# Dense stage and fourth pass of a four-layer graph network: reciprocal roots by one power instruction on GpSimd, and a sum moved within DVE's unit

## Chip, cores and metric

One core of a Trainium2 chip runs the whole program. The metric is the device time of one execution in microseconds, the median of several runs. Engines: PE (TensorE), DVE (VectorE), ACT (ScalarE), POOL (GpSimd) and SP (SyncE, which here only issues DMAs). All run their own instruction streams in order and meet at semaphores.

## What is computed

Four graph layers on 50000 nodes of 256 features and 25000 edges, each x = x + layer(relu(layernorm(x))). Layer 0 is two graph attention layers, layer 1 dot-product attention over edges, layer 2 a hyperbolic attention layer, layer 3 a two-step graph convolution. Cut to what the change touches:

```
def _layernorm(x, eps=1e-05):
    return (x - mean(x)) / sqrt(var(x) + eps)
...
# layer 2
h_dir = h_raw / maximum(norm(h_raw), 1e-12)
h_mag = sigmoid(x @ mag_w.T + mag_b) * 1.5
h = h_dir * h_mag
...
h_combined = h + agg                      # agg: softmax-weighted sum over the edges of a node
un_c = maximum(norm(h_combined), 1e-15)
h_poincare = tanh(un_c) * h_combined / un_c     # then clipped to norm 0.95
```

A reciprocal root is thus needed per row: of the layernorm's variances, and of the squared norm of h_raw and of h_combined.

## The kernel before

**The dense stage** (from line 613) treats every node as if it had no incoming edge, so that all four layers become products of rows; nodes with edges are mended afterwards. It goes over the nodes in 98 units (U = 98) of 512 rows (G = 4 rows for each of 128 partitions). It is a software pipeline: in unit n of an engine's stream, `a`, `z`, `b`, `c`, `d`, `e`, `f` are the units n, n-1, ... n-6, each at a later step of the network. `hold(engine, semaphore, value, ...)` is a wait. Each engine's unit is written out in a fixed order.

- DVE, unit n (the inner `unit`, lines 998 to 1050 or so): oo of n-6 (L1004: x3o plus a constant row, the result of nodes without edges, into its own buffer); bn_stats of xin of unit n+1 (L948, the x statistics); `scales` of n-5, which waits for ACT's tanh (reciprocals from L202 on), and x3o (L1013); em (L1018); g (L1023); two evacuations into f2o (L995), x1 (L1031) and its bn_stats (L1035); the squared norms into var (L955, which waits for ACT's squares); then `statistics` (the variance, L221 to L229, and `rsqrt`, eleven operations L150 to L163, between which the two evacuations into f1o are woven, also L995); `shifts` (nm, L967, which ACT's layernorms wait for); `norms` (L177 to L192, up to unc, which the tanh reads).
- `rsqrt` (lines 146 to 165) makes a first value by an integer shift and subtraction and improves it in three steps of three operations. It writes rt, 12 values for each partition here; ACT takes rt as its scale, with nm as its bias. Its last step scales by ROOT = 16, since var holds the sum and not the mean of the squares.
- ACT: h1 of n (L885, the first reader of nm and rt), the copy hr (L895), zm (L900), the turned copies tt (L874), tanh of n-5 (L906), exp (L909), h2 of n-3 (L914), squares of n-4 (L923), ho (L932).
- PE: transposes (L820) and products (L830) for three of the steps.
- POOL, unit n: for n < 28 an iota and seven indirect DMAs into PLACE (`scatter_places`, L779 and L784), afterwards six small gathers (`find_places`, L796); then `fetch_targets`, two gathers of rows of x into xd (L768), which wait until the XD store of unit n-2 has landed.
- SP, unit n, in this order, each entry behind its own wait: store F1 of n-1 (waits for f1o), store HL of n-6 (ho), store `out` of n-6 (oo), store X3 of n-5 (x3o), store H2 of n-3, store F2 of n-2 (f2o), load xin of unit n+2 (L700: waits until h1 and x1 of unit n-2 have freed the slot; there are four), store XD of n-2 (L740). The stores are of 512 to 528 KB, XD's of 256 KB, the load of 512 KB. The core lines of SP's unit:

```
j = at.back(6)
...
    hold(sp, s["oo"], j.n + 1, ps)
    sp.dma_start(view, flat(oo, j.slot, np_)).then_inc(o_out[j.slot], 16)
...
if at.back(-2).alive(U):
    load(at.back(-2))
```

**The fourth pass** (from line 2183) goes over the 25088 padded edges in 28 groups of seven tiles of 128 and computes the softmax-weighted sums of layer 2. POOL gathers group n's rows of HL (seven indirect DMAs, L1318, into one of three slots); the gather of n waits until PE has accumulated group n-3. DVE, group n: lg (L2306, waits for the gathered rows), crow and the selection (L1438) of n-1, two scans (L1386, L1388) of n, then for n-3 var (L2324), `rsqrt` and unc (L2326), then hc of n-2 (L2336), the differences of n, and the output of n-3 (L2350), which waits for ACT's tanh of unc. PE, ACT and SP serve the same groups.

Of the kernel before, what the change touches and what calls it, by code (L numbers as in the profile page):

```python
# [172 lines left out]
def magnitude(nc, link, fac, e, r, un, unc, n2):  # L173
# [11 lines left out]
    n = link.go(V.scalar_tensor_tensor(fac, fac, 1.5 / ROOT, r, ALU.mult, ALU.mult))  # L185
    yield
    link.need(n)
    if un is not None:
        n = link.go(V.tensor_tensor(un, un, fac, ALU.mult))
        yield  # L190
        link.need(n)
        n = link.go(V.tensor_scalar(unc, un, 1.0 / ROOT, 1e-15, ALU.mult, ALU.max))  # L192
        yield
        link.need(n)
# [20 lines left out]
def layernorm_stats(nc, link, st, mean, dm, var):  # L215
# [15 lines left out]
    link.need(n)  # L231


def gnn_program(nc, x, src, dst, edge_weight, W1, a_src1, a_dst1, b1, W2, a_src2, a_dst2, b2,
# [36 lines left out]
    with ctx:  # L271
# [341 lines left out]
        with Phase() as ph:  # L613
# [16 lines left out]
            var, ra = ph.sb("var", [P, 3 * G]), ph.sb("ra", [P, 3 * G])  # L630
# [19 lines left out]
                "f1_h", "f2_h", "hr_h", "em", "sq", "x1", "unc", "tanh", "x3", "ho", "oo", "warm", "pad", "low", "edge")}  # L650
# [39 lines left out]
            with nc.Block() as block:  # L690
# [61 lines left out]
                def _(pool):  # L752
                    pp = ph.passed["pool"]
                    nc.gpsimd.memset(ho[:, :, :, 258:F2W], 1.0)
                    nc.gpsimd.iota(low_i[:, :], [[1, 1]], base=N - P, channel_multiplier=1)
                    nc.gpsimd.memset(warm[:, :], 0.0).then_inc(s["pad"], 1)
# [43 lines left out]

                    def unit(at):
                        if at.n < NS:
                            scatter_places(at.n)
                        else:
                            find_places(at.n - NS)
                        fetch_targets(at.n)
                    unrolled(pool, U, 0, unit)
# [130 lines left out]
                def _(dve):  # L938
# [18 lines left out]
                    def statistics(at):  # L957

                        yield from layernorm_stats(nc, link, st, mean[:, :], dm[:, :], var[:, 0:2 * G])
                        hold(dve, s["h1_h"], min_int(at.n * 2, 2 * U), pv)  # L960
                        hold(dve, s["h2"], min_int(at.n - 3, U), pv)
                        yield from rsqrt(nc, link, rt[:, at.slot, :], var[:, :], ra[:, :], ROOT)

                    def shifts(at):

                        if at.back(-1).alive(U) or at.back(2).alive(U):
# [3 lines left out]
                    def norms(at):  # L970
# [5 lines left out]
                                             un[:, :], unc[:, :], n2[:, d.slot, :])  # L976
# [11 lines left out]
                    take(statistics(At(-1, -1, 3, 4)))  # L988
# [9 lines left out]
                    def unit(at):  # L998
                        a, z, b, c, d, e, f = (at.back(k) for k in range(7))
                        link.restart()  # L1000
                        if f.alive(U):
                            hold(dve, s["x3"], f.n + 1, pv)
                            hold(dve, o_out[f.slot], 16 * f.use, pv)
                            V.tensor_tensor(oo[:, f.slot, :, :], x3o[:, f.slot, :, :], wide(gcn_const, D, G),  # L1004
                                            ALU.add).then_inc(s["oo"], 1)
# [503 lines left out]
        def within(n):  # L1509
            return 0 <= n < NS  # L1510
# [672 lines left out]
        with SoftPass(1, 1, 259, (HL, 7), None, X3) as ph:  # L2183
            ph.step("scaled", "hc", "sq", "unc", "tanh", "tiles_turned", "tile_sums", "sums_turned", "tile_carry", "carry_turned",
# [6 lines left out]
            var, ra, rt = ph.sb("var", [P, GS]), ph.sb("ra", [P, GS]), ph.sb("rt", [P, GS])  # L2191
# [67 lines left out]
            with nc.Block() as block:  # L2259
                @block.gpsimd  # L2260
                def _(pool):
                    ph.start_pool(pool)
# [5 lines left out]
                    every(0, group)  # L2268
# [25 lines left out]
                def _(dve):  # L2294
# [5 lines left out]
                    def group(n):  # L2300
# [464 lines left out]
```

## Time and profile before

| | us |
|---|---|
| median of 3 runs | 5989.73 |
| lowest, highest run | 5988.09, 6006.96 |
| span of the profiled execution (its own device time is not listed apart) | 5993.1 |
| PE busy in the span | 4608.6 (77%) |
| DVE busy | 4603.5 (77%) |
| POOL busy | 3500.3 (58%) |
| ACT busy | 2965.7 (49%) |

The profile is of one execution; its times are microseconds from the start of the span. "L995" is line 995. Busy time excludes waits and the issuing of DMAs by SP. In a row of the timeline stand the start, the duration, the engine, the line and operation, the tiles (out<-in) with their sizes, how many instructions were merged (x4), and in brackets how long the engine had been idle before and what released it. SPq rows are DMA issues: their duration is the issue, not the transfer.

### The profile page before, as it was taken

How to read it: one execution, taken by the hardware profiler on the slowest of the kernel's cores; microseconds unless marked ns; L12 is line 12 of the kernel's file. 1: busy time of each engine (PE TensorE's matmuls, PEld its weight loads, DVE VectorE, ACT ScalarE, POOL GpSimd, SP SyncE). 2: the span in 40 equal slices, each digit the busy share in tenths (PEclk: the TensorE clock that was granted, in tenths of full speed). 3: DMA queues.
4: the chain of work that ended last, by engine and by line, in shares of the span. 5: the costliest groups of instructions: out<-in, count | busy, mean ns of one | idle time of the engine just before them, and what ended most of it. 6: DMA issues, size and time to landing. Idle time of an engine off the chain costs nothing. (4 is left out here: it accounts for less than half of the span.)

```text
span 5993.1 us, 77451 instructions
## 1 busy us (share of the span) xinstructions
PE 4608.6 (77%) x21160; PEld 3351.9 (56%) x21160; DVE 4603.5 (77%) x13478; ACT 2965.7 (49%) x7524; POOL 3500.3 (58%) x3009
## 2 busy tenths in 40 slices
PE   3888888888884888865777778888857674887887
PEld 3666666666663666643565545555534443665555
DVE  5888888888886888847999647777768887985554
ACT  2777777777772444432444435555545552331111
POOL 3555445454524767728888278777725433546777
PEclk9999999999996999987888889999978887998998
DMA  3666666667663444425777535555536774554444
GB/s 119 239 242 247 237 243 241 244 242 244 240 236 128 125 123 129 128 71 174 256 243 250 200 110 155 147 151 155 154 103 217 249 241 151 169 159 132 140 156 130
DMA packets 651621, 1096.83 MB, mean 183 GB/s; under 512 B 88390, under 2 KB 471814, under 8 KB 651069
## 3 DMA queue, kind: packets, MB, share of 16 engines
q1 hardware_dynamic: 525754, 837.10, 41.0%
q0 software_dynamic: 125440, 254.79, 14.7%
q8 instruction: 176, 2.88, 0.2%
q14 instruction: 251, 2.06, 0.1%
HBM read 523.88 MB, written 575.95 MB: 184 GB/s over the span
## 5 line engine op out<-in xcount | busy, mean ns | idle before, releaser
L830 PE MATMUL mm<-w,tt 128*128 128x264 f32 x3136 | 736.9, 389 | 0.8 <-ACT tt L874 0.8
L830 PEld LDWEIGHTS mm<-w,tt 128*128 128x128 f32 x3136 | 585.5, 192 | 92.5 <-ACT tt L874 1.0
L1318 POOL DMA_INDIRECT aim<-F,index x392 | 551.7, 1407 | 119.5 <-issue 119.2
L768 POOL DMA_INDIRECT xd<-in_x_dram,index x196 | 218.4, 1114 | 676.0 <-DMA XD<-xd 645.1
L1318 POOL DMA_INDIRECT got<-F,index x392 | 491.9, 1255 | 204.7 <-issue 111.2
L1476 ACT ACTIVATE rows<-acc 128x260 f32<-128x260 f32 (+1 forms) x588 | 227.4, 387 | 623.4 <-PE acc L1467 623.4
L796 POOL DMA_INDIRECT place<-PLACE,place_ix x392 | 425.2, 1085 | 119.5 <-issue 119.5
L820 PE MATMUL tp<-ident,h 128*128 128x128 f32 x1568 | 236.8, 284 | 323.9 <-ACT h L914 162.0
L1463 PE MATMUL acc<-got,sel 128*128 128x260 f32 (+1 forms) x1176 | 425.8, 449 | 74.8 <-DVE sel L1438 68.2
L2487 DVE SCALAR_TENSOR_TENSOR agg<-mask,agg,acc 128x128 f32<-128x128 f32 x784 | 251.8, 343 | 253.5 <-PE acc L2474 144.2
L830 PE MATMUL mm<-wl,tt 128*128 128x264 f32 x1568 | 419.4, 389 | 6.0 <-ACT tt L874 5.8
L820 PEld LDWEIGHTS tp<-ident,h 128*128 128x128 f32 x1568 | 167.5, 141 | 426.5 <-ACT h L885 224.3
L1208 PE MATMUL kv<-wkv,ht 128*128 128x512 f32 x784 | 384.9, 615 | 0.1
L885 ACT ACTIVATE h<-xin,nm,rt 128x256 f32<-128x256 f32 x392 | 203.3, 589 | 325.2 <-DVE nm L967 325.2
L874 ACT ACTIVATE tt<-tp 128x512 f32<-128x512 f32 x588 | 314.4, 585 | 79.3 <-PE tp L820 79.3
L1467 PE MATMUL acc<-rows,carry 128*128 128x260 f32 (+1 forms) x1008 | 345.0, 426 | 7.9 <-ACT rows L1476 1.7
L1318 POOL DMA_INDIRECT got<-HL,index x196 | 216.0, 1102 | 225.9 <-PE acc L1467 173.3
L1376 PE MATMUL turned<-ident,top 128*4 128x128 f32 (+1 forms) x588 | 124.9, 380 | 283.0 <-DVE top L1368 151.5
L1463 PEld LDWEIGHTS acc<-got,sel 128*128 128x128 f32 x1176 | 250.2, 225 | 142.4 <-DVE sel L1438 82.2
L2738 ACT ACTIVATE yt<-m,b_col 128x512 f32<-128x512 f32 x98 | 67.5, 689 | 504.4 <-PE m L2714 504.4
L830 PEld LDWEIGHTS mm<-wl,tt 128*128 128x128 f32 x1568 | 260.5, 192 | 83.2 <-issue 9.2
L2442 POOL DMA_INDIRECT got<-X,index x196 | 196.6, 1003 | 180.5 <-ACT h L2609 134.7
(348 smaller groups left out, 13645.7 us busy)
## 6 DMA issues: line engine op xcount, KB each, us to landing
F<-f1o SPq DMA_DIRECT2D x97, 528.0 KB
F<-f2o SPq DMA_DIRECT2D x97, 528.0 KB, 3.4
HL<-ho SPq DMA_DIRECT2D x97, 528.0 KB, 3.7
xin<-in_x_dram SPq DMA_DIRECT2D x97, 512.0 KB
H<-h SPq DMA_DIRECT2D x97, 512.0 KB, 3.7
X<-x3o SPq DMA_DIRECT2D x97, 512.0 KB
out_dram<-oo SPq DMA_DIRECT2D x97, 512.0 KB
drow<-DSTF SPq DMA_DIRECT2D x84, 448.0 KB
```

The costliest lines, as they stand in the source:

```text
L768: nc.gpsimd.indirect_dma_start(out=xd[:, n % 2, t, :], out_offset=None, in_=x, in_offset=bass.IndirectOffsetOnAxis(ap=index[:, tile, 1:2], ...
L796: nc.gpsimd.indirect_dma_start(out=place[:, t, k:k + 1], out_offset=None, in_=cells, in_offset=bass.IndirectOffsetOnAxis(ap=place_ix[:, t, ...
L820: last = nc.tensor.transpose(bank[:, 2 * r + k, :], rows_t[:, 2 * q + r, k * P:(k + 1) * P], ident[:, :])
L830: last = nc.tensor.matmul(mm[PAIR[stage, q]][:, r, 0:F2W], lhs[:, q, 2 * r + k, :], w[:, k, :], start=(k == 0), stop=(k == KB - 1))
L874: nc.scalar.activation(tt[k][:, q, :, :], tp[q][:, :, :], ACT.Copy).then_inc(s["t_h"], 1)
L885: relu = nc.scalar.activation(h1[:, r, :], xin[:, a.slot4, r, :], ACT.Relu, bias=nm[:, last_turn, r:r + 1], scale=rt[:, last_turn, r:r + 1])
L1208: last = nc.tensor.matmul(acc, lhs[:, k, :], w[:, k, :], start=(k == 0), stop=(k == KB - 1))
L1318: nc.gpsimd.indirect_dma_start(out=buf[:, n % SLOTS, t, :], out_offset=None, in_=table, in_offset=bass.IndirectOffsetOnAxis(ap=index[:, n ...
L1463: nc.tensor.matmul(acc, self.sel[:, s, t, :], self.got[:, n % SLOTS, t, 0:w], start=True, stop=False)
L1467: nc.tensor.matmul(acc, self.carry[:, s, t * P:(t + 1) * P], self.rows[:, s, t - 1, :] if t else self.crow[:, :], start=False, stop=True)\
L1476: nc.scalar.activation(self.rows[:, n % 2, t, :], self.acc[tile % 2][:, 0:self.width], ACT.Copy)\
L2487: last = nc.vector.scalar_tensor_tensor(self.agg[:, sl, k, t * P:(t + 1) * P], self.mask[:, sl, t, :], before, self.acc[sl][:, t, k, :], A ...
```

## The change

In the dense stage and in the fourth pass `rsqrt` goes. DVE signals a new semaphore `var` when the variances stand; POOL has a tile `half` of -0.5 and computes rt = var ^ -0.5 by one tensor_tensor instruction with the operation pow (128 x 12 values in the dense stage, 128 x 7 in the fourth pass), and signals `root`, for which DVE waits before nm (dense stage) or unc (fourth pass). In the dense stage a `variance` function gives the mean of the squares in place of their sum, so the factor ROOT becomes 1. oo moves from the head of DVE's unit to behind the f1o evacuations, ahead of nm; SP's stream stays as it is. POOL's `roots(n)` stands between its place work and `fetch_targets`, and in the fourth pass the power of group n-3 stands behind gather(n).

```diff
+def variance(nc, link, st, mean, dm, var, ready):
+    V = nc.vector
+    V.tensor_tensor(mean, st[:, :, 1], st[:, :, 4], ALU.add)
+    n = link.go(V.tensor_tensor(dm, st[:, :, 1], st[:, :, 4], ALU.subtract))
+    link.go(V.scalar_tensor_tensor(var, st[:, :, 2], D * 1e-5, st[:, :, 5], ALU.add, ALU.add))
+    link.need(n)
+    n = link.go(V.scalar_tensor_tensor(dm, dm, 0.25, dm, ALU.mult, ALU.mult))
+    link.need(n)
+    V.scalar_tensor_tensor(var, var, 1.0 / D, dm, ALU.mult, ALU.add).then_inc(ready, 1)
...
 # dense stage, POOL
+                    nc.gpsimd.memset(half[:, :], -0.5)
...
+                    def roots(n):
+                        hold(pool, s["h1_h"], min(n * 2, 2 * U), pp)
+                        hold(pool, s["h2"], min(n - 3, U), pp)
+                        hold(pool, s["var"], n + 2, pp)
+                        nc.gpsimd.tensor_tensor(rt[:, n % 2, :], var[:, :], half[:, :], ALU.pow).then_inc(s["root"], 1)
+
                     def unit(at):
                         if at.n < NS:
                             scatter_places(at.n)
-                        else:
+                        elif at.n < U:
                             find_places(at.n - NS)
+                        roots(at.n)
                         fetch_targets(at.n)
-                    unrolled(pool, U, 0, unit)
+                    roots(-1)
+                    unrolled(pool, U, 6, unit)
...
 # dense stage, DVE
-                    def statistics(at):
-                        yield from layernorm_stats(nc, link, st, mean[:, :], dm[:, :], var[:, 0:2 * G])
+                    def statistics():
+                        variance(nc, link, st, mean[:, :], dm[:, :], var[:, 0:2 * G], s["var"])
+
+                    def shifts(at):
                         hold(dve, s["h1_h"], min_int(at.n * 2, 2 * U), pv)
                         hold(dve, s["h2"], min_int(at.n - 3, U), pv)
-                        yield from rsqrt(nc, link, rt[:, at.slot, :], var[:, :], ra[:, :], ROOT)
-                    def shifts(at):
+                        hold(dve, s["root"], at.n + 2, pv)
...
                     def unit(at):
                         a, z, b, c, d, e, f = (at.back(k) for k in range(7))
                         link.restart()
-                        if f.alive(U):
-                            hold(dve, s["x3"], f.n + 1, pv)
-                            hold(dve, o_out[f.slot], 16 * f.use, pv)
-                            V.tensor_tensor(oo[:, f.slot, :, :], x3o[:, f.slot, :, :], wide(gcn_const, D, G),
-                                            ALU.add).then_inc(s["oo"], 1)
                         if at.back(-1).alive(U):
                             x_stats(at.back(-1))
...
-                        steps = statistics(at)
+                        statistics()
                         if a.alive(U):
                             hold(dve, f1_out[a.slot], 16 * a.use, pv)
                             for q in range(2):
-                                take(steps, 5)
                                 evacuate(a, "a", "mma_h", f1o[:, a.slot, :, 0:F2W], rb1, "f1_h", q)
-                        take(steps)
+                        if f.alive(U):
+                            hold(dve, s["x3"], f.n + 1, pv)
+                            hold(dve, o_out[f.slot], 16 * f.use, pv)
+                            V.tensor_tensor(oo[:, f.slot, :, :], x3o[:, f.slot, :, :], wide(gcn_const, D, G),
+                                            ALU.add).then_inc(s["oo"], 1)
                         shifts(at)
...
 # fourth pass, POOL
                     def group(n):
                         if within(n):
                             ph.gather(pool, n, 0, bound, d["acc"], (n - 2) * GS)
-                    every(0, group)
+                        c = n - 3
+                        if within(c):
+                            hold(pool, d["unc"], c, None)
+                            hold(pool, d["var"], c + 1, None)
+                            nc.gpsimd.tensor_tensor(rt[:, :], var[:, :], half[:, :], ALU.pow).then_inc(d["root"], 1)
+                    every(3, group)
...
 # fourth pass, DVE
-                            link(V.tensor_scalar(var[:, :], n2[:, c % 2, :], 1e-30, None, ALU.max))
-                            take(rsqrt(nc, link, rt[:, :], var[:, :], ra[:, :]))
-                            V.tensor_tensor(unc[:, :], var[:, :], rt[:, :], ALU.mult).then_inc(d["unc"], 1)
+                            V.tensor_scalar(var[:, :], n2[:, c % 2, :], 1e-30, None, ALU.max).then_inc(d["var"], 1)
...
                             hold(dve, d["hc"], x + 1, None)
                             dve.sem_inc(d["used"], 1)
+                        if within(c):
+                            hold(dve, d["root"], c + 1, None)
+                            V.tensor_tensor(unc[:, :], var[:, :], rt[:, :], ALU.mult).then_inc(d["unc"], 1)
```

## Rows read from the trace of the kernel before

**Rows 1.** The page: busy time of each engine (share of the span).

```profile
PE 4608.6 (77%) x21160; PEld 3351.9 (56%) x21160; DVE 4603.5 (77%) x13478; ACT 2965.7 (49%) x7524; POOL 3500.3 (58%) x3009
```

**Rows 2.** Busy time by stretch: PE, PEld, DVE, ACT, POOL; then clock, DMA share, GB/s.

```profile
600.00:1200.00 600.00, 492.40 (x2586) 390.28 (x2585) 511.95 (x1736) 456.87 (x1089) 297.75 (x274) 1.00 0.69 242
...
4530.00:4980.00 450.00, 297.61 (x1160) 190.28 (x1159) 392.26 (x1155) 226.27 (x786) 177.82 (x162) 0.79 0.72 236
```

**Rows 3.** Timeline of one dense unit, ACT and DVE.

```profile
1001.15 2.07 ACT L885 ACTIVATE h<-xin,nm,rt 128x256 f32<-128x256 f32 x4 [3.27 <-DVE nm L967]
...
1002.59 1.24 DVE L1004 TENSOR_TENSOR oo<-x3o,gcn_const 128x1024 f32<-128x1024 f32 x1 [0.36 <-DVE unc L192]
...
1006.01 0.20 ACT L906 ACTIVATE th<-unc 128x4 f32<-128x4 f32 x1
...
1006.25 0.18 DVE L202 RECIPROCAL gb<-unc 128x4 f32<-128x4 f32 x1 [1.11 <-ACT th L906]
...
1015.07 0.17 DVE L229 TENSOR_TENSOR var<-dm,var 128x8 f32<-128x8 f32 x1
...
1015.56 0.70 DVE L995 TENSOR_TENSOR f1o<-mm,rb 128x528 f32<-128x528 f32 x1
...
1018.51 0.17 DVE L967 SCALAR_TENSOR_TENSOR nm<-mean,rt 128x8 f32<-128x8 f32 x1
```

**Rows 4.** Timeline, DVE: oo of the unit 34 units earlier.

```profile
401.75 1.23 DVE L1004 TENSOR_TENSOR oo<-x3o,gcn_const 128x1024 f32<-128x1024 f32 x1 [0.36 <-DVE unc L192]
```

**Rows 5.** Timeline of SP's queue in the same unit.

```profile
1003.85 0.34 SPq L719 DMA_DIRECT2D out_dram<-oo  x1
1009.22 0.32 SPq L724 DMA_DIRECT2D X<-x3o  x1
...
1012.97 0.33 SPq L700 DMA_DIRECT2D xin<-in_x_dram  x1
1013.34 0.63 SPq L740 DMA_DIRECT2D XD<-xd  x1
```

**Rows 6.** GpSimd: groups by line (busy us, mean ns, idle before), and one timeline row.

```profile
L1318 POOL DMA_INDIRECT got<-HL,index x196 | 216.0, 1102 | 225.9 <-PE acc L1467 173.3 <-issue 51.8 <-DVEq L1308 0.8
L784 POOL DMA_INDIRECT PLACE<-edge_row,index x196 | 209.5, 1069 | 59.4 <-issue 51.3 <-POOL edge_row L779 8.1
...
L755 POOL IOTA low_i<- 128x1 int32 x1 | 0.1, 134 | 0.0
...
1019.52 1.00 POOL L768 DMA_INDIRECT xd<-in_x_dram,index  x1 [6.95 <-DMA XD<-xd]
```

**Rows 7.** Busy time by stretch, columns as in rows 2: two single microseconds.

```profile
1002.00:1003.00 1.00, 0.65 (x4) 0.42 (x4) 0.64 (x2) 1.00 (x3) 0.69 (x2) 1.00 1.00 410
1009.00:1010.00 1.00, 0.82 (x8) 0.83 (x9) 1.00 (x3) 0.81 (x4) 0.81 (x1) 1.00 0.02 1
```

**Rows 8.** Timeline of the first load and its reader; landing of XD's stores (L740's view).

```profile
75.69 1.30 SPq L700 DMA_DIRECT2D xin<-in_x_dram  x3
...
79.24 1.41 DVE L948 BATCH_NORM_STATS2 st<-xin 128x6 f32<-128x256 f32 x4 [3.23 <-DMA xin<-in_x_dram]
...
DMA to landing us min/median/max: 3.2/5.2/5.9
```

**Rows 9.** Timeline of the fourth pass, POOL and DVE.

```profile
4509.62 1.00 POOL L1318 DMA_INDIRECT got<-HL,index  x1 [7.61 <-PE acc L1467]
...
4518.87 1.24 POOL L1318 DMA_INDIRECT got<-HL,index  x1 [0.30 <-issue]
...
4523.28 0.17 DVE L2306 TENSOR_TENSOR lg<-got,aim_score 128x7 f32<-128x7 f32 x1 [1.31 <-DMA got<-HL,index]
...
4540.24 0.17 DVE L2306 TENSOR_TENSOR lg<-got,aim_score 128x7 f32<-128x7 f32 x1 [0.18 <-issue]
4546.45 0.13 DVE L2324 TENSOR_SCALAR var<-n 128x7 f32<-128x7 f32 x1
```

**Rows 10.** Line 2324 (var of the fourth pass): durations, first and last start.

```profile
L2324 DVE TENSOR_SCALAR var<-n x28: 132/132/173, 4528.9 to 4972.0; 128x7 f32<-128x7 f32 x28
```

More of the change, by code:

```diff
@@ L170, in min_int, with magnitude @@
     return min(value, most) if type(value) is int else value
-def magnitude(nc, link, fac, e, r, un, unc, n2):
+def magnitude(nc, link, fac, e, r, un, unc, n2, root=ROOT):
     V = nc.vector
@@ L184, in magnitude @@
     link.need(n)
-    n = link.go(V.scalar_tensor_tensor(fac, fac, 1.5 / ROOT, r, ALU.mult, ALU.mult))
+    n = link.go(V.scalar_tensor_tensor(fac, fac, 1.5 / root, r, ALU.mult, ALU.mult))
     yield
@@ L191, in magnitude @@
         link.need(n)
-        n = link.go(V.tensor_scalar(unc, un, 1.0 / ROOT, 1e-15, ALU.mult, ALU.max))
+        n = link.go(V.tensor_scalar(unc, un, 1.0 / root, 1e-15, ALU.mult, ALU.max))
         yield
@@ L629, in gnn_program @@
             mean, dm = ph.sb("mean", [P, 2 * G]), ph.sb("dm", [P, 2 * G])
-            var, ra = ph.sb("var", [P, 3 * G]), ph.sb("ra", [P, 3 * G])
+            var, half = ph.sb("var", [P, 3 * G]), ph.sb("half", [P, 3 * G])
             rt, nm = ph.sb("rt", [P, 2, 3 * G]), ph.sb("nm", [P, 2, 2 * G])
@@ L649, in gnn_program @@
                 "ch", "stats", "h1_h", "h2", "zm", "exp", "g", "tp_h", "t_h", "mma_h", "mmb_h", "mmc_h",
-                "f1_h", "f2_h", "hr_h", "em", "sq", "x1", "unc", "tanh", "x3", "ho", "oo", "warm", "pad", "low", "edge")}
+                "f1_h", "f2_h", "hr_h", "em", "sq", "x1", "unc", "tanh", "x3", "ho", "oo", "warm", "pad", "low", "edge", "ones", "var", "root")}
             def rows_of(table, at):
@@ L975, in norms @@
                         yield from magnitude(nc, link, fac[:, d.slot, :], em[:, d.slot, :], rt[:, at.slot, 2 * G:3 * G],
-                                             un[:, :], unc[:, :], n2[:, d.slot, :])
+                                             un[:, :], unc[:, :], n2[:, d.slot, :], 1.0)
                     def scales(e):
@@ L987, in _ @@
                     link.restart()
-                    take(statistics(At(-1, -1, 3, 4)))
+                    statistics()
                     shifts(At(-1, -1, 3, 4))
@@ L1037, in unit @@
                         link.restart()
-                        steps = statistics(at)
+                        statistics()
                         if a.alive(U):
@@ L2183, in gnn_program @@
         with SoftPass(1, 1, 259, (HL, 7), None, X3) as ph:
-            ph.step("scaled", "hc", "sq", "unc", "tanh", "tiles_turned", "tile_sums", "sums_turned", "tile_carry", "carry_turned",
+            ph.step("scaled", "hc", "sq", "var", "root", "unc", "tanh", "tiles_turned", "tile_sums", "sums_turned", "tile_carry", "carry_turned",
                     "filled", "filled_turned")
@@ L2190, in gnn_program @@
             den, n2, th = ph.sb("den", [P, GS]), ph.sb("n2", [P, 2, GS]), ph.sb("th", [P, GS])
-            var, ra, rt = ph.sb("var", [P, GS]), ph.sb("ra", [P, GS]), ph.sb("rt", [P, GS])
+            var, half, rt = ph.sb("var", [P, GS]), ph.sb("half", [P, GS]), ph.sb("rt", [P, GS])
             unc = ph.sb("unc", [P, GS])
@@ L2261, in _ @@
                 def _(pool):
+                    nc.gpsimd.memset(half[:, :], -0.5)
                     ph.start_pool(pool)
```

## The prediction, made before the change was run

> **What bounds the kernel now.** I read the engine totals first: DVE and TensorE are each busy 77% of the span and no engine is full, so no sum of busy time decides [rows 1]. Next the busy times by stage. The dense stage (about 79 to 1860 us) repeats one unit 98 times plus a few to fill and drain; between 600 and 1200 us DVE is busy 512 of 600 us, and in the fourth pass (about 4480 to 4980) 392 of 450 [rows 2]. There DVE is nearly the bound, so the waits around it matter. The third view is one unit in order of time [rows 3]. It shows a loop of two engines. ACT waits 3.27 us for nm, the shifts that end DVE's unit. From its first operation behind nm (1001.15) ACT works without a pause to the tanh, which ends at 1006.21: 5.1 us. DVE waits 1.11 us for it and then works from 1006.25 to the next nm at 1018.51. The eleven root operations and the two f1o evacuations (0.70 each) stand in the 3.27 us between var's end (1015.24) and nm. oo, the sum that the change moves, stands just behind the norms, at 1002.59, where it and the x statistics fill the time until the tanh. From the oo of 401.75 to that of 1002.59 are 34 units: 17.67 us each [rows 4, 3].
>
> The view of SP's own queue is the fourth and decides the forecast [rows 5]. SP works in order. In its unit n it stores F1 and HL, waits for oo of this same unit n of DVE (the out store, n-6), and only behind that stores X3, H2 and F2, **loads xin for unit n+2**, and stores XD. Now out goes at 1003.85, early in the unit, and the load at 1012.97, when x1 has freed its slot. DVE unit n+1 begins with the statistics of exactly that load.
>
> **The change in the dense stage.** (1) Eleven root operations leave DVE. (2) oo comes between f1o and nm. What stands between var and nm becomes two evacuations of 0.70 and oo with 1.23 (0.70 + 0.70 + 1.23 = 2.63), against 3.27: 0.64 us less per unit, if nothing else moves. DVE behind nm is left with norms and statistics and waits longer for the tanh, which costs nothing as that is ACT's chain. (3) The power on GpSimd runs beside these 2.63 us. No row shows it. Its lower bound is 0.13 us, GpSimd's smallest iota; an indirect DMA's issue, which works through 128 rows, takes 1.07 to 1.10 [rows 6]; nothing excludes several times that for a transcendental function, so I set 4 us as the upper end, my choice, four times that issue. I take 1.0, near the indirect DMA's issue, as that row too is more than a memory write. In the dense stage it is free up to 2.6 us. GpSimd reaches it in time: at unit n its place gathers are issued by 1012.6, var ends at 1015.24, and GpSimd waits for XD's store until 1019.52 anyway (its row has 6.95 us of wait) [rows 3, 6].
>
> (4) The queue that oo is moved past is SP's. The out store now waits for the end of DVE's unit, and X3, H2, F2, the xin load and XD all stand behind it, though their data is ready. Call the end of oo T. The issues are 0.37 us apart [rows 5], so the load is issued at T + 1.5, about where nm is. Four stores go ahead of it into the DMA engines. The X3 store that was issued at 1009.22 left the engines idle until about 1009.97 (their share is 0.02 in the microsecond from 1009), and full engines move some 400 GB/s (410 in the microsecond from 1002) [rows 5, 7], so 528 KB take 1.3 us. The engines begin at T + 0.75 and are through the four stores at T + 0.75 + 5.2 = T + 5.95. The load's own data and receipt: the first load of the stage, issued at 75.69, let DVE start at 79.24, so 3.55 us of which 0.75 before data moves, 2.8. In the steady units XD, issued 0.37 behind the load, lands at a median of 5.2 [rows 8], 5.6 behind the load's issue; less some 1.3 for XD's own 256 KB in small rows the load lands 4.3 behind its issue, and some 0.8 of that is the wait for F2's data ahead of it: 3.5 or less. I take 3.35: **the load lands at T + 9.3** (bounds 8.2 to 10.5). Then: statistics 1.4 [rows 8], 0.1 to the first reciprocal, and from there (1006.25) to var's end (1015.24) 8.99, then 2.63. The new loop is 9.3 + 1.4 + 0.1 + 8.99 + 2.63 = **22.4 us against 17.67, 4.75 more**. It holds where there is both an out store and a load, units 6 to 95: 90 x 4.75 = +428 us. The 14 units around them gain 0.64 each, -9.
>
> Does something else then bind? XD lands 1.3 to 2 behind the load, at about T + 11, GpSimd's two target gathers take 2.6 more, its seven scatters of the first 28 units (1.07 and 0.3 of issue each) and their iota 9.9 [rows 6]: it reaches the next power at T + 23.5, 1.1 us behind the next oo. nm would be late by some 2 us, but the tanh (5.1 behind nm) is still ready before the statistics at the next T + 10.7. TensorE keeps its 14.5 us of work a unit (492.4 over 34) [rows 2]. So no.
>
> **The change in the fourth pass.** Eleven operations of 0.2 us leave each of 28 groups (2.2 us). But GpSimd's group n issues gather(n), then waits for var of DVE's group n, then the power, and only then gather(n+1). Today gathers run ahead, held only by TensorE's accumulation: at 4509.62 one starts that way, its seventh issue is at 4518.87 and DVE's lg had to wait for the data until 4523.28 [rows 9]. Now gather(n+1) starts behind var of group n, and group n+1 begins with lg. From lg to var's end are 6.34 us (4540.24 to 4546.58), power 1.0, from the first of seven issues to the last 8.75 (six steps of 1.10 and 0.30 are 8.4 [rows 6], the row's case with one slow one has 9.25), landing behind the last 4.4 (4518.87 to 4523.28): 20.5 us against a mean of 16.41 (var from 4528.9 to 4972.0 over 27 intervals) [rows 9, 10]. 24 gathers (4 to 27) are held: 24 x 4.1 = +98. Bounds: with a landing of 2.8 (the first load's above) and a power of 0.13, 18.0 a group, +39; with 4 us of power +170. The last groups have no gather and gain 2 us each, -6. The new waits in DVE's group stand behind 3.4 us of hc and cost nothing.
>
> **Sum.** +428 - 9 + 98 - 6 = +511. The profile's span is 5993.1, 3.4 above the median of 5989.7, less than the 0.3% (18 us) that a measurement here tells from no change; against the median I forecast 6500.
>
> **What the Trainium skill adds.** Row and page on the DMA: "DMA: Bandwidth & Descriptors", on the anatomy of one DMA, gives some 2.0 us fixed plus bytes over 436 GB/s. That is, as an estimate, T + 8.0 for four stores and a load, and the sum would be about 117 us smaller. The first load's 3.55 us agrees with its 3.2 within 0.4. On the power: "GPSIMD Engine Reference", performance versus the Vector engine, has elementwise work on GpSimd at about half DVE's speed, which speaks against moving it; twice the 0.17 us of a DVE root operation would make the fourth pass 16 us shorter than my sum.
>
> **Rivals.** (a) The load does not queue behind the stores' data and lands as it does in the steady units, about 4.3 after its issue, T + 5.9. The loop is then 5.9 + 13.1 = 19.0, +1.35 x 90 = +122, in all 6195. For it: reads and writes are different traffic. Against it: XD, half the size, lands at a median of 5.2 behind the load and at 3.2 at its quickest [rows 8]. 9%.
> (b) The power takes about 4 us and holds oo back, since both read SBUF: oo ends at var + 5.2 in place of + 2.63, 2.6 x 90 = +234, and the fourth pass 3 x 24 = +72: 6805. It decides from 1.4 us, when f1o is done and oo would start; its point is that oo then delays SP's queue too. Whether GpSimd and DVE hold each other up so, no row of this kernel shows, and its price is unseen. 7%. "SBUF — State Buffer", on who interferes with whom, states such a lock between a DVE operation with two SBUF inputs and a GpSimd operation that reads SBUF; f1o reads PSUM and is not concerned.
> (c) Faster: SP's queue costs nothing, the load lands before the tanh is ready anyway. For this it must land by T + 3.7, 2.2 us after its issue. Then -0.64 x 98 = -63; if the gathers of the fourth pass also stay ahead, 28 x 2.2 = -62: 5865. Against it: the shortest landing of an XD store is 3.2, and the first load, with nothing ahead, took 3.55 [rows 8]. 3%.
> (d) Parts of both cancel (small dense loss, gather loss alone), within 0.3%: 2%.
>
> **How the numbers follow.** My forecast, 6500, holds 79%. Its range adds the ends of the load's landing (-1.1 and +1.2 us x 90 = -99 and +108) and of the fourth pass (-59 and +72, power included): 6342 to 6680. With a part of (b) above and the coarse rates below I give 6340 to 6700; (a) and (c) lie outside. Faster 0.03, same 0.02, slower 0.95.
>
> **What would show it.** After: nm to nm 22.4 us in the dense stage (units 6 to 95), the x statistics (L948 now) waiting for the DMA of xin, 5 us or so in each, in place of the wait for the tanh; SP's out, X3, H2, F2, xin and XD issued within 2.5 us at the end of DVE's unit; the engines idle for nearly half the unit; the power under 2.6 us. In the fourth pass: lg waiting for got, and gathers whose first issue follows the power, groups of about 20.5. Units below 19.5 us would make the queueing wrong; a power above 2 us the price; nm still waited for by ACT at 17 us a unit, the whole argument.

## The result: slower by 9.5%, and the profile after

The changed kernel took a median of 6566.61 us (6558.91 to 6571.59, 4 runs), the kernel before beside it 5991.31: a ratio of 1.095, 95% interval 1.0935 to 1.0966. The forecast was 6500 in a range of 6340 to 6700.

The page of the profiled execution, engine totals, against [rows 1]:

```profile
PE 4777.6 (73%) x21160; PEld 3452.8 (53%) x21160; DVE 4359.9 (66%) x12015; ACT 2967.0 (45%) x7524; POOL 3831.4 (58%) x3144
```

DVE did 244 us less work, GpSimd 331 more, and the kernel is 577 us longer: the time went into waits. The busy times of the stretch from 600 to 1200 us, as in [rows 2], show DVE down from 512 to 356 of 600 us (TensorE's granted clock fell from 1.00 to 0.91 in it; in the view of waits from 200 to 2200 us DVE waits for PE nowhere, so the lower clock doesn't set the unit):

```profile
600.00:1200.00 600.00, 442.73 (x2044) 340.78 (x2042) 356.11 (x1077) 359.41 (x859) 317.45 (x249) 0.91 0.53 190
```

The last oo of the dense stage starts at 2273.4 us, before it was 1851.1: 422 us later. The fourth pass adds the rest. The view of oo's line and of var's line in the fourth pass, after (count, durations, first and last start), against [rows 10]:

```profile
L1064 DVE TENSOR_TENSOR oo<-x3o,gcn_const x98: 1212/1216/1223, 190.3 to 2273.4; 128x1024 f32<-128x1024 f32 x98
...
L2351 DVE TENSOR_SCALAR var<-n x28: 132/133/172, 4943.1 to 5550.8; 128x7 f32<-128x7 f32 x28
```

A group of the fourth pass is (5550.8 - 4943.1) / 27 = 22.51 us long, before 16.41, together +165 us. With the 422 that is 587, ten more than the whole, which the other stages give back.

The timeline of one dense unit after, the counterpart of [rows 3] and [rows 5], with SP's issues between DVE's and GpSimd's work (T is the end of oo, as in the prediction):

```profile
1003.54 1.41 DVE L971 BATCH_NORM_STATS2 st<-xin 128x6 f32<-128x256 f32 x4 [5.57 <-DMA xin<-in_x_dram]
...
1013.68 0.17 DVE L244 SCALAR_TENSOR_TENSOR var<-var,dm 128x8 f32<-128x8 f32 x1
1013.76 1.32 DVE L1018 TENSOR_TENSOR f1o<-mm,rb 128x528 f32<-128x528 f32 x2
1014.12 1.01 POOL L810 DMA_INDIRECT place<-PLACE,place_ix  x1 [0.30 <-DVE var L244]
1015.00 1.22 DVE L1064 TENSOR_TENSOR oo<-x3o,gcn_const 128x1024 f32<-128x1024 f32 x1
1015.15 3.21 POOL L820 TENSOR_TENSOR rt<-var,half 128x12 f32<-128x12 f32 x1
1016.24 0.34 SPq L732 DMA_DIRECT2D out_dram<-oo  x1
1016.62 0.43 SPq L737 DMA_DIRECT2D X<-x3o  x1
1017.10 0.78 SPq L742 DMA_DIRECT2D H<-h  x1
1017.92 1.18 SPq L747 DMA_DIRECT2D F<-f2o  x1
1018.50 0.17 DVE L990 SCALAR_TENSOR_TENSOR nm<-mean,rt 128x8 f32<-128x8 f32 x1 [2.29 <-POOL rt L820]
...
1019.20 1.14 SPq L713 DMA_DIRECT2D xin<-in_x_dram  x1
...
1020.38 1.20 SPq L753 DMA_DIRECT2D XD<-xd  x1
...
1026.16 1.40 DVE L971 BATCH_NORM_STATS2 st<-xin 128x6 f32<-128x256 f32 x4 [6.58 <-DMA xin<-in_x_dram]
```

The reader sees the queue. oo ends at 1016.22 (T). SP issues its store and right behind it four transfers that waited for nothing but their turn. The load is the fifth in the row, goes out at T + 2.98, and the statistics that read it begin at 1026.16, T + 9.94, after 6.58 us of waiting. One loop is 22.6 us (1003.54 to 1026.16). This unit is longer than most: over the 88 units whose statistics start between 176 and 2139 us the mean is 22.3 us, and from T to the statistics the median is 9.35 us, 3.0 to the load's issue and 6.4 from there. Before, a unit is 17.6 us by the same measure.

The transfers' data starts only behind T. The DMA share, last column but one, of two single microseconds of this unit (columns as in [rows 2]); between them, from 1017 on, it is 0.94 or more in each:

```profile
1016.00:1017.00 1.00, 0.86 (x5) 0.33 (x3) 0.21 (x1) 0.00 (x0) 1.00 (x1) 1.00 0.01 0
1025.00:1026.00 1.00, 1.00 (x5) 0.54 (x3) 0.00 (x0) 1.00 (x3) 0.00 (x0) 1.00 1.06 426
```

Two views of waits say the same for the stretch from 200 to 2200 us, DVE's and SP's own (us in total, times, longest):

```profile
DVE st L971 <- DMA xin<-in_x_dram: 539.2, 90, 8.6
...
DVE nm L990 <- POOL rt L820: 220.5, 90, 4.6
```

```profile
SPq L732 <- DVE oo L1064: 1387.6, 90, 17.5
```

The second line looks like a second price, the power that nm waits for. The tanh, 5.1 us behind nm, is ready at about 1023.8, before the statistics can even start. And oo, at which SP's queue starts, doesn't wait for the power. So that wait costs nothing here; the experiments show when it begins to.

The fourth pass after, one group:

```profile
5202.39 0.13 DVE L2351 TENSOR_SCALAR var<-n 128x7 f32<-128x7 f32 x1
...
5202.68 1.52 POOL L2294 TENSOR_TENSOR rt<-var,half 128x7 f32<-128x7 f32 x1 [12.13 <-DVE var L2351]
...
5204.39 1.08 POOL L1339 DMA_INDIRECT got<-HL,index  x1 [0.19 <-issue]
...
5212.50 0.37 SPq L2314 DMA_DIRECT2D xe<-XE  x1
...
5212.85 1.00 POOL L1339 DMA_INDIRECT got<-HL,index  x1 [0.30 <-issue]
...
5220.52 0.17 DVE L2333 TENSOR_TENSOR lg<-got,aim_score 128x7 f32<-128x7 f32 x1 [8.06 <-DMA got<-HL,index]
```

GpSimd is idle for 12 us until var, takes the power, then issues seven gathers, and DVE starts its next group 7.7 us after the last of them was issued (median of 19 groups: 7.4). SP's next transfers (xe, the X3 store, drow) go out at the very time of that last issue.

### The profile page after: what moved, and what is told of

Its sections match the earlier page's. It is cut to its first block and busy times, and to the rows that moved or that the text cites. A ratio compares the mean times of both kernels' runs of the same rounds, so it can differ in the third digit from the quotient of the medians.

```text
span 6569.8 us, 76354 instructions
## 1 busy us (share of the span) xinstructions
PE 4777.6 (73%) x21160; PEld 3452.8 (53%) x21160; DVE 4359.9 (66%) x12015; ACT 2967.0 (45%) x7524; POOL 3831.4 (58%) x3144
## 3 DMA queue, kind: packets, MB, share of 16 engines
q14 instruction: 242, 1.98, 0.1%
## 5 line engine op out<-in xcount | busy, mean ns | idle before, releaser
L853 PE MATMUL mm<-w,tt 128*128 128x264 f32 x3136 | 877.3, 436 | 192.1 <-DVE f2o L1018 191.8
L853 PEld LDWEIGHTS mm<-w,tt 128*128 128x128 f32 x3136 | 660.8, 219 | 346.3 <-issue 226.1
L843 PE MATMUL tp<-ident,h 128*128 128x128 f32 x1568 | 269.3, 315 | 365.0 <-ACT h L908 289.1
L971 DVE BATCH_NORM_STATS2 st<-xin 128x6 f32<-128x256 f32 x392 | 137.7, 414 | 544.1 <-DMA xin<-in_x_dram 542.6
L843 PEld LDWEIGHTS tp<-ident,h 128*128 128x128 f32 x1568 | 192.8, 157 | 462.6 <-ACT h L908 352.3
L820 POOL TENSOR_TENSOR rt<-var,half 128x12 f32<-128x12 f32 x105 | 302.3, 2879 | 74.2 <-DVE var L244 72.4
L1397 PEld LDWEIGHTS turned<-ident,top 128*4 128x4 f32 (+1 forms) x588 | 58.1, 107 | 503.2 <-DVE top L2336 309.8
```

Source lines behind the costliest of these rows:

```text
L820: nc.gpsimd.tensor_tensor(rt[:, n % 2, :], var[:, :], half[:, :], ALU.pow).then_inc(s["root"], 1)
L843: last = nc.tensor.transpose(bank[:, 2 * r + k, :], rows_t[:, 2 * q + r, k * P:(k + 1) * P], ident[:, :])
L853: last = nc.tensor.matmul(mm[PAIR[stage, q]][:, r, 0:F2W], lhs[:, q, 2 * r + k, :], w[:, k, :], start=(k == 0), stop=(k == KB - 1))
```

## Experiments

Theory A after the result: the dense loss is SP's queue behind the late oo, the fourth pass's is GpSimd's gathers behind var. Rival B: the power itself, 2.3 to 3.2 us on GpSimd, makes the loss. Rival C: DVE's own order. Each ratio is to the kernel before on the same chip, which takes 5998 us beside e1 to e4 and 5996 beside e5 to e8. e9, e10 and e11 ran on a chip where it takes 6059 us, so they are compared by their ratios. Medians of units or groups below are read from the timelines of 85 to 90 dense units, or of 18 or 19 groups in the middle of the fourth pass, which are longer than the mean over all 27 intervals (before: 16.9 against 16.4 us).

**e1_oo_head: the changed kernel, oo back at the head of DVE's unit.**

```diff
+                        if f.alive(U):
+                            hold(dve, s["x3"], f.n + 1, pv)
+                            hold(dve, o_out[f.slot], 16 * f.use, pv)
+                            V.tensor_tensor(oo[:, f.slot, :, :], x3o[:, f.slot, :, :], wide(gcn_const, D, G),
+                                ALU.add).then_inc(s["oo"], 1)
                         if at.back(-1).alive(U):
                             x_stats(at.back(-1))
...
-                        if f.alive(U):
-                            hold(dve, s["x3"], f.n + 1, pv)
-                            hold(dve, o_out[f.slot], 16 * f.use, pv)
-                            V.tensor_tensor(oo[:, f.slot, :, :], x3o[:, f.slot, :, :], wide(gcn_const, D, G),
-                                ALU.add).then_inc(s["oo"], 1)
                         shifts(at)
```

> The changed kernel with one part undone: oo back at the head of DVE's unit, the powers stay on GpSimd. Theory A (SP's queue behind oo makes the dense loss): units fall from 22.6 us to 17.2 or less, as the load is issued in mid-unit again; the fourth pass keeps its 22.5 us a group, so about 5991 + 166 - 50 = 6110 us. The power should take 2.3 us without oo beside it, nm waits for it behind f1o for about 1 us. Rival B (the power on GpSimd, late or slow, makes the dense loss): units stay above 21 us and the time above 6450.

Measured: 6081.61 us, ratio 1.0139 (1.012 to 1.0159): 485 us less than the changed kernel. The timeline of its unit, from var to oo:

```profile
1006.12 0.17 DVE L244 SCALAR_TENSOR_TENSOR var<-var,dm 128x8 f32<-128x8 f32 x1
1006.20 1.32 DVE L1018 TENSOR_TENSOR f1o<-mm,rb 128x528 f32<-128x528 f32 x2
1006.46 2.30 POOL L820 TENSOR_TENSOR rt<-var,half 128x12 f32<-128x12 f32 x1 [2.85 <-DVE var L244]
...
1008.89 0.17 DVE L990 SCALAR_TENSOR_TENSOR nm<-mean,rt 128x8 f32<-128x8 f32 x1 [1.38 <-POOL rt L820]
...
1014.20 0.18 DVE L202 RECIPROCAL gb<-unc 128x4 f32<-128x4 f32 x1 [1.25 <-ACT th L929]
```

nm starts 2.60 us behind var's end, before 3.27 [rows 3], and DVE waits for the tanh again and no longer for the load (4.7 us of idle ahead of all 392 statistics). The first loads of the two kernels differ by 1 us at most, and the last oo starts at 1798.9, before 1851.1: the powers alone make the dense stage some 52 us shorter. Units are 16.9 us, within the expectation; the total is 28 us under it. Rival B is wrong.

**e2_out_last: the changed kernel, the out store as the last issue of SP's unit.**

```diff
-                            view, np_ = rows_of(out, j)
-                            hold(sp, s["oo"], j.n + 1, ps)
-                            sp.dma_start(view, flat(oo, j.slot, np_)).then_inc(o_out[j.slot], 16)
...
                                 .then_inc(xd_out[j.slot], 16)
+                        j = at.back(6)
+                        if j.alive(U):
+                            view, np_ = rows_of(out, j)
+                            hold(sp, s["oo"], j.n + 1, ps)
+                            sp.dma_start(view, flat(oo, j.slot, np_)).then_inc(o_out[j.slot], 16)
```

> The changed kernel, oo late in DVE's unit, but SP issues the out store as the last of its unit, behind the load and XD. Theory A: the late oo itself is harmless, only the stores and the load queued behind it are dear; units 17.5 to 18.2 us, about 6130 to 6210 us in all with the fourth pass as it is. If a power that is under way holds oo back (both read SBUF), the power takes 2.3 us from var, oo comes behind it, nm about 3.8 us behind var: units 18.2. If not, nm is 3.3 or less behind var: units 17.6. Rival B (power): above 21 us a unit. Rival C (the late oo delays DVE itself, not SP): units above 20.

Measured: 6095.82 us, ratio 1.0168 (1.0149 to 1.0186). DVE's and GpSimd's streams are the changed kernel's own; the place of one store in SP's order is worth 471 us. That shows the queue, and against rival C that a late oo costs DVE nothing. The same stretch of its unit:

```profile
1004.40 0.17 DVE L244 SCALAR_TENSOR_TENSOR var<-var,dm 128x8 f32<-128x8 f32 x1
...
1004.75 2.30 POOL L822 TENSOR_TENSOR rt<-var,half 128x12 f32<-128x12 f32 x1 [2.85 <-DVE var L244]
1005.72 1.22 DVE L1066 TENSOR_TENSOR oo<-x3o,gcn_const 128x1024 f32<-128x1024 f32 x1
1006.96 0.34 SPq L757 DMA_DIRECT2D out_dram<-oo  x1
1007.18 0.17 DVE L992 SCALAR_TENSOR_TENSOR nm<-mean,rt 128x8 f32<-128x8 f32 x1 [0.24 <-POOL rt L822]
```

oo starts while the power is under way and takes its usual 1.22 us: the power does not hold oo back. nm comes 2.61 us behind var's end. The total was 34 us under the expected span, as the units did not reach 17.5 but 16.9.

**e3_move_only: the kernel before, with oo moved and nothing else.**

```diff
                         take(steps)
+                        if f.alive(U):
+                            hold(dve, s["x3"], f.n + 1, pv)
+                            hold(dve, o_out[f.slot], 16 * f.use, pv)
+                            V.tensor_tensor(oo[:, f.slot, :, :], x3o[:, f.slot, :, :], wide(gcn_const, D, G),
+                                ALU.add).then_inc(s["oo"], 1)
                         shifts(at)
```

> The kernel before with one part of the change alone: oo moved behind f1o and the last root operation, ahead of nm; roots stay on DVE. Theory A: the whole dense loss and a little more, since the eleven operations stay in the loop: units of 22.6 + 0.64 = 23.2 us, 90 x 5.5 = +500, about 6490 us; the fourth pass unchanged at 16.4 us a group. Rival B: close to 5991, at most + 120 (1.2 us a unit of oo in the path).

Measured: 6603.31 us, ratio 1.1013 (1.0987 to 1.1039), 113 us more than expected. Its last oo starts at 2458.5: the dense stage grew by 607 us, not by 500. The mechanism is the expected one, only larger, with the statistics waiting for the load:

```profile
1014.60 0.34 SPq L719 DMA_DIRECT2D out_dram<-oo  x1
...
1017.57 1.16 SPq L700 DMA_DIRECT2D xin<-in_x_dram  x1
...
1023.61 1.40 DVE L948 BATCH_NORM_STATS2 st<-xin 128x6 f32<-128x256 f32 x4 [8.07 <-DMA xin<-in_x_dram]
```

From these starts (statistics at 999.70 and 1023.61) a unit is 23.9 us, the median is 24.1; its load lands at T + 9.0. The expected 23.2 had a wrong sum behind it: it added the 0.64 us by which 3.27 (roots and evacuations) is longer than 2.63 (evacuations and oo). But here oo stands behind the 3.27, not in their place. From the statistics to the end of oo are 14.9 us (median) against 12.7 in the changed kernel: 2.2 us more a unit, over 90 units some 200 us, which is the step from 422 to 607 within 15 us.

**e4_fourth_only: the kernel before, with the fourth pass of the change.** Its diff is the fourth-pass half of the change above.

> The kernel before with only the fourth pass changed. If the parts add up: dense unchanged, the fourth pass at 22.5 us a group, 5991 + 166 = 6157 us. If part of the fourth pass's loss came from the dense stage's new timing (a later start, another clock), less than 6130.

Measured: 6146.06 us, ratio 1.025 (1.0226 to 1.0275), +148 us. Its groups are (5127.6 - 4529.9) / 27 = 22.14 us long. The parts add up: the 422 us of the dense stage and these 148 make 570, and the changed kernel is 575 us longer than the one before. The end of one of its groups:

```profile
4721.76 1.00 POOL L1318 DMA_INDIRECT got<-HL,index  x1 [0.31 <-issue]
4721.79 0.36 SPq L2293 DMA_DIRECT2D xe<-XE  x1
...
4728.56 0.17 DVE L2312 TENSOR_TENSOR lg<-got,aim_score 128x7 f32<-128x7 f32 x1 [6.79 <-DMA got<-HL,index]
```

**e6_gate_only: the kernel before, GpSimd waits for var but takes no power.**

```diff
                             ph.gather(pool, n, 0, bound, d["acc"], (n - 2) * GS)
-                    every(0, group)
+                        c = n - 3
+                        if within(c):
+                            hold(pool, d["var"], c + 1, None)
+                    every(3, group)
...
                             link(V.tensor_scalar(var[:, :], n2[:, c % 2, :], 1e-30, None, ALU.max))
+                            dve.sem_inc(d["var"], 1)
```

> The kernel before with one thing added in the fourth pass: GpSimd waits behind gather(n) for var of group n-3, as in the change, but takes no power; the roots stay on DVE. Theory A (the place of the wait costs, not the power): the group is 22.5 less the power's 1.5 = 21.0 us, 5998 + 24 x 4.6 = 6108 us. Rival (the power costs): close to 5998.

Measured: 6025.36 us, ratio 1.0051 (1.0033 to 1.007), +30 us where 110 were expected. Groups of (5007.3 - 4529.7) / 27 = 17.69 us. Both sides were wrong: the gate costs 1.3 us a group, and the power's 1.5 us alone cannot make up the other 4.4. The timeline shows what differs from e4:

```profile
4720.93 1.00 POOL L1318 DMA_INDIRECT got<-HL,index  x1 [0.30 <-issue]
4723.06 0.36 SPq L2290 DMA_DIRECT2D xe<-XE  x1
...
4724.37 0.17 DVE L2309 TENSOR_TENSOR lg<-got,aim_score 128x7 f32<-128x7 f32 x1 [1.34 <-DMA got<-HL,index]
```

Here the last gather is issued 2.1 us ahead of SP's xe, the first of its transfers of 2.2 MB, and its data is used 3.44 us after its issue. In e4 the two coincide and it is 6.8. What closes the 2.1 us is mostly the power. Counted from lg (medians), the last gather is issued at 14.8 us in e6 and at 16.4 in e4, where the power of 1.51 us stands ahead of the gathers; xe goes out at 16.8 in e6 and at 16.3 in e4, where DVE's group has lost its eleven operations.

**e9_burst_waits: e4, and SP holds xe, the X3 store, drow and carry until the next group's gathers have landed.** Against e4:

```diff
+                        if within(n + 1):
+                            ph.gathered(sp, n + 1)
                         if within(c):
                             hold(sp, d["put"], c, None)
```

> e4_fourth_only (the fourth pass of the change alone, 22.1 us a group) with one wait more on SP: its burst of xe, the X3 store, drow and carry waits until the gathers of the next group have landed. Theory A (the gathers' late landing, 6.8 us behind the last issue in place of e6's 3.4, is the burst's data in the same DMA engines): the landing falls to 3.4 us and the group to 18.8 to 19.2 us, about 6070 us. Rival (the power or the issue itself makes the landing late): 22 us a group, 6146 us.

Measured: ratio 1.0083 (1.0058 to 1.0108) against e4's 1.025; groups of (5043.9 - 4539.6) / 27 = 18.68 us. Its last gather and the next lg:

```profile
4724.51 1.00 POOL L1318 DMA_INDIRECT got<-HL,index  x1 [0.30 <-issue]
4727.34 0.36 SPq L2295 DMA_DIRECT2D xe<-XE  x1
4727.34 0.17 DVE L2314 TENSOR_TENSOR lg<-got,aim_score 128x7 f32<-128x7 f32 x1 [3.61 <-DMA got<-HL,index]
```

2.83 us from issue to use (median 2.9, in e4 7.1). Everything ahead of that is as in e4: from lg to var's end 6.35 us, to the first gather 8.2, to the last 16.5 (e4: 16.4), so the other chip doesn't explain the difference. So of the 5.7 us that e4's group is longer than before, 3.5 are the collision with SP's transfers (22.14 - 18.68) and 1.3 the gate (e6). The remaining 1.0 is a difference between e9 and e6: the power's 1.5 us less a landing that is 0.6 us shorter than e6's. The shares hold for this order of undoing; no run holds the burst back with the gate alone.

**e7_lag_alone: the fourth pass's power one group later in GpSimd's stream, dense stage of before.** Against e4:

```diff
-                        c = n - 3
+                        c = n - 4
...
-                    every(3, group)
+                    every(4, group)
```

> The kernel before with the fourth pass's roots on GpSimd, one group later in its stream. Theory A: no loss, and DVE, busy most of the group, gives back part of the 2.2 us of its eleven operations: 14.6 to 16.4 us a group, 5945 to 5998 us.

Measured: 5995.55 us, ratio 1.0002 (0.9992 to 1.0011). The loss is gone, and nothing is gained: the groups are (4968.9 - 4525.6) / 27 = 16.42 us long. The waits from 4530 to 5000 us say where DVE's 2.2 us went:

```profile
DVE wt L1411 <- PE back L1403: 65.7, 25, 2.9
```

DVE now waits 2.6 us a group for PE's results, which stand behind the accumulations in PE's order; before it is 0.4 us. DVE was 87% busy in that stretch [rows 2], but its operations lay beside a chain of PE and ACT of the same length.

**e5_head_and_lag: both repairs, e1's dense stage and e7's fourth pass.**

> oo at the head of DVE's unit as in e1_oo_head, and in the fourth pass GpSimd takes the power one group later in its stream (behind gather(n) that of group n-4), so that the gathers stay ahead. Theory A (both losses are queues: SP's behind oo, GpSimd's gathers behind var): the dense stage keeps e1's gain of some 60 us, the fourth pass is at 15 to 16.4 us a group: 5900 to 5935 us, faster than both kernels. Rival (the gathers were late through the power's own time): the groups stay above 19 us, 6000 or more.

Measured: 5939.1 us, ratio 0.9908 (0.9893 to 0.9923), faster than both kernels and 4 us over the expected span. Its last oo starts at 1796.6, 54.5 us earlier than before; the fourth pass, with groups of (4914.3 - 4471.2) / 27 = 16.41 us, gives nothing.

**e8_split_power: e5 with the dense power in two instructions.** Against e5:

```diff
-                        nc.gpsimd.tensor_tensor(rt[:, n % 2, :], var[:, :], half[:, :], ALU.pow).then_inc(s["root"], 1)
+                        for part in (slice(0, 2 * G), slice(2 * G, 3 * G)):
+                            nc.gpsimd.tensor_tensor(rt[:, n % 2, part], var[:, part], half[:, part],
+                                                    ALU.pow).then_inc(s["root"], 1)
...
-                        hold(dve, s["root"], at.n + 2, pv)
+                        hold(dve, s["root"], at.n * 2 + 3, pv)
...
+                        hold(dve, s["root"], at.n * 2 + 4, pv)
                         if d.alive(U):
                             take(norms(at))
```

> e5 with the dense power in two instructions, first the eight variances that nm waits for, then the four norms. If the power's time goes by its columns (1.5 us for 7, 2.3 us for 12 so far), nm comes some 0.6 us earlier behind var, 98 x 0.6 = 59 us less than e5. If each power has a large fixed cost or the last norms then end the unit, no gain against e5.

Measured: 5888.92 us, ratio 0.9817 (0.9804 to 0.9831), 50 us less than e5 where 59 were expected, and the best version. Its powers by shape (busy us, mean ns), and nm:

```profile
L821 POOL TENSOR_TENSOR rt<-var,half 128x8 f32<-128x8 f32 x105 | 175.1, 1667 | 221.1 <-DVE var L244 221.1
L821 POOL TENSOR_TENSOR rt<-var,half 128x4 f32<-128x4 f32 x105 | 105.8, 1008 | 0.0
```

```profile
1009.22 0.17 DVE L244 SCALAR_TENSOR_TENSOR var<-var,dm 128x8 f32<-128x8 f32 x1
...
1011.37 0.17 DVE L992 SCALAR_TENSOR_TENSOR nm<-mean,rt 128x8 f32<-128x8 f32 x1 [0.74 <-POOL rt L821]
1012.26 0.17 DVE L177 TENSOR_SCALAR fac<-em 128x4 f32<-128x4 f32 x1 [0.73 <-POOL rt L821]
```

nm starts 1.98 us behind var's end, 0.6 less than in e1; the second part delays only the norms, which have time until the tanh.

**e10_oo_with_power: e2 with oo ahead of the f1o evacuations, so that it has begun when the power starts.** The edit moves the four lines of oo to behind `statistics()`.

> e2_out_last (units of 16.9 us, power 2.30 us) with oo ahead of the f1o evacuations, so that oo is under way when the power begins. Theory A (a GpSimd operation that reads SBUF waits for a DVE operation with two SBUF inputs that began first): the power takes 3.2 us as in the changed kernel, nm comes 0.9 us later, units 17.8 us, about 6180 us. Rival (the long power of the changed kernel had another cause, as GpSimd's preceding gathers): power 2.3 us, 6096 us.

Measured: ratio 1.0269 (1.024 to 1.0299) against e2's 1.0168. Units of 17.73 us (nm at 1010.11 and 1027.84; in e2 16.9). oo and the power:

```profile
1006.59 1.22 DVE L1062 TENSOR_TENSOR oo<-x3o,gcn_const 128x1024 f32<-128x1024 f32 x1
1006.85 3.12 POOL L822 TENSOR_TENSOR rt<-var,half 128x12 f32<-128x12 f32 x1 [2.82 <-DVE var L244]
```

The power takes 3.12 us, 0.82 more than in e2 where it began first.

**e11_load_first: the changed kernel, SP's load ahead of the out store, stores and XD still behind it.**

```diff
+                        if at.back(-2).alive(U):
+                            load(at.back(-2))
+                        if j.alive(U):
                             view, np_ = rows_of(out, j)
                             hold(sp, s["oo"], j.n + 1, ps)
...
-                        if at.back(-2).alive(U):
-                            load(at.back(-2))
```

> The changed kernel with SP's load of xin ahead of the out store, the stores and XD still behind it. Theory A: the statistics no longer wait for DMA. If nothing else binds, units of 16.9 us as in e2 and 6096 us. But XD is still late: it lands some 8.5 us behind oo, GpSimd's gathers take 10.7 more and the power 2.3 to 3.2, so nm comes 22 us behind the oo of a unit before, and 16.7 us after nm comes the next oo but one: a loop of 38.7 us over two units, 19.4 a unit, 6096 + 90 x 2.4 = 6310 us. I expect this second one.

Measured: ratio 1.0531 (1.0463 to 1.0598). The statistics no longer wait for DMA, and a second queue binds: XD late, GpSimd's gathers late, and the power at 1006.74, 4.6 us behind var. oo starts at 986.38, 1003.31 and 1024.68: units of 16.9 and 21.4 in turn, 19.2 on the mean, as the expected loop over two units says. The mean over all units, (2023.8 - 193.9) / 97 = 18.9, is 0.5 under the expected 19.4, partly as the units at both ends are short. The ratio is the expected one: 6310 over 5998 is 1.052.

## Why the prediction was right

**The dense stage, step by step.** Predicted +419 us, measured 422 at the last oo; units of 22.4, measured 22.3 on the mean. (4), SP's queue, is shown by e2, where DVE and GpSimd do the same and only SP's order differs, and by e3, where the move alone makes the loss. Its terms: the load was to be issued at T + 1.5 and went at T + 3.0, since four issues in a row take 0.34, 0.43, 0.78 and 1.18 us and not 0.37 each, a distance that the prediction took from a single pair; it was to land 7.8 behind its issue and did so 6.4 behind (medians). The two errors cancel, T + 9.3 against T + 9.35, and that the dense stage came out within 3 us is luck to that extent; the mechanism is not. The rest of the loop, 13.1 in the prediction, took 12.7 (1003.54 to the end of oo at 1016.22). The Trainium skill's "DMA: Bandwidth & Descriptors" (anatomy of one DMA), whose figures gave the estimate T + 8.0, is 1.4 us low at the median and 1.9 in the unit shown; its fit is for one DMA issued from GpSimd, and these are five in a row from SP.

(1) and (2), 0.64 us less a unit if nothing else moves, came out as e1: nm 2.60 us behind var against 3.27. But not through oo's and the evacuations' 2.63: there the power sets it.

(3), the power, was put at 1.0 us; it takes 2.30 for 12 values, and 3.21 in the changed kernel. The interval up to 4 held it, but by the prediction's own sign, a power above 2 us, its price was wrong. It was free in the dense stage, though not because it fits beside 2.6 us: nm comes 4.7 us behind var's end (median), and what pays for it is the other reason given, that the tanh is ready before the load.

**The fourth pass.** Predicted +92, measured +165: groups of 22.5 and not 20.5. The gate is there, and two of the four terms hold (lg to var's end 6.3 us, first to last issue 8.5 where 8.75 stood). The power is 1.5 and not 1.0, and the landing is the term that was mis-sized: 7.7 against 4.4. I took it from one gather of the kernel before. e9 shows that the difference is the collision with SP's burst, with 3.5 us a group, and that with it gone the landing is 2.8. What brings them together is a consequence of the change that the prediction did not draw: the power delays the last gather by 1.6 us behind lg, and SP's transfers go 0.5 us earlier, as DVE's group has lost eleven operations (e6 against e4). This term, with the power's 0.5 us, is why the total came 67 us above the forecast, inside its range. The sentence that DVE is nearly the bound there was wrong too: e7 takes the eleven operations, 2.2 us, away without loss and gains nothing, as PE's accumulations end last.

**The rivals.** (a), a load that is issued late but does not queue behind the stores' data, is out by its own numbers: it had the load land 4.3 us behind its issue and units of 19.0, and measured are 6.4 and 22.3, with the DMA engines busy from the stores' first data to the landing. e2 doesn't decide this, since it takes the wait away and the burst with it. How the 2.1 us above 4.3 divide between the stores' data, the transfers issued behind the load and the load's own longer issue (1.15 us where it is 0.33 before, medians), no run separates. (b) had the lock the wrong way round: in e2 oo starts inside the power and is not held; in e10 and in the changed kernel the power starts inside oo and takes 0.8 to 0.9 us more. "SBUF — State Buffer" of the Trainium skill (who interferes with whom) says that the one that starts first blocks the other fully; the trace agrees for a power behind oo and not for oo behind a power, and the measurement decides. (c) would have needed a load within 2.2 us. "GPSIMD Engine Reference" of the Trainium skill (performance versus the Vector engine) has its factor of about two from an add of 2048 columns. The estimate made from it, twice a DVE operation's 0.17 us, is far below the 2.30 us measured for a power of 12; its direction holds, though eleven operations of DVE, 2.2 us in their chain, are about one power.

## What to carry to other kernels

When an operation moves later on its engine, look at the queue of the engine that waits for it: here one store waits for a sum, and a load that has nothing to do with it stands four places behind. Moving the store in the issuing order was worth 471 us, and the same power that stood in a losing change wins 1.8% when oo is back in its place, its wait in the fourth pass lies beside other work and its input in the dense stage is split so that the first consumer waits for its part alone. Before counting an engine's removed work as gain, ask which wait of that engine replaces it; at 87% busy DVE gave nothing back.

## What the runs showed of the hardware

- A power of GpSimd on 128 partitions took 1.01, 1.51, 1.67 and 2.30 us for 4, 7, 8 and 12 values: by a line through these, some 0.16 us for each further value and 0.4 us besides.
- A power that began while DVE's oo (both inputs in SBUF) was under way took 3.12 to 3.21 us, against 2.30; oo, begun during a power, kept its 1.22 us.
- SP's issues became longer in a burst: 0.34, 0.43, 0.78, 1.18, 1.14 and 1.20 us for six in a row, where issues that stood apart mostly took 0.3 to 0.5.
- Where 2.2 MB of SP's transfers were issued at the time of the last of seven gathers, that gather's data was used 7.1 us after its issue (7.4 in the changed kernel), and 2.9 us after it where SP held them back (medians).
